# Four graph layers in one kernel: the third layer multiplies by its weights first, in fp32r halves, and by the triangles of the adjacency last

## What is computed

```python
def _layernorm(x, axis=-1, eps=1e-05):
    m = jnp.mean(x, axis=axis, keepdims=True)
    v = jnp.var(x, axis=axis, keepdims=True)
    return (x - m) / jnp.sqrt(v + eps)

def _L2_gnn_ref(x, W, adj, bias):
    adj_0 = jnp.diag(jnp.diagonal(adj))
    adj_1 = jnp.triu(adj, k=1)
    adj_2 = jnp.tril(adj, k=-1)
    h = jnp.einsum('bjf,kfo->kbjo', x, W)
    out = jnp.einsum('ij,bjo->bio', adj_0, h[0]) + jnp.einsum('ij,bjo->bio', adj_1, h[1]) + jnp.einsum('ij,bjo->bio', adj_2, h[2])
    return out + bias[None, None, :]
...
    h = jnp.maximum(_layernorm(x, axis=-1), 0.0)
    x = x + _L2_gnn_ref(h, L2_gnn_W, adj, L2_gnn_bias)
```

## Time and profile before

| | |
|---|---|
| median of three runs | 1389.29 us (1384.57 to 1389.65) |
| profiled execution | 1389.11 us, span 1387.3 us |
| busy PE / PEld / DVE / ACT / POOL over the span | 91% / 81% / 74% / 58% / 31% |
| third layer | from 912.7 to 1073.0 us of the span |

### The profile page before, as it was taken

One profiled execution on the slowest core, in us unless ns is written; L12 is line 12 of the kernel. 1 busy time (PEld: TensorE's weight loads), 2 busy tenths in 40 slices (PEclk: granted clock), 3 DMA queues, 4 the chain that ended last, 5 costly groups with the idle time before them and its releaser, 6 DMA issues. The chain is left out here.

```text
span 1387.3 us, 27428 instructions
## 1 busy us (share of the span) xinstructions
PE 1268.5 (91%) x8454; PEld 1123.1 (81%) x8454; DVE 1020.0 (74%) x2911; ACT 802.8 (58%) x1756; POOL 436.9 (31%) x546
## 2 busy tenths in 40 slices
PE   2899999999999999999997999979999899997998
PEld 2778787787877878778786877869998799985998
DVE  6677877778777787777875999967775688856675
ACT  3575775756757577575775777722221677752332
POOL 3121312213112131121311222268885333312332
PEclk7899999999999999999999999999999899987999
DMA  9200000000000000000000000000000000000222
GB/s 273 69 1 1 1 1 0 0 0 0 0 0 0 0 0 0 0 0 1 0 1 0 1 0 0 1 1 0 0 0 1 0 0 0 0 1 23 76 68 76
DMA packets 24696, 20.72 MB, mean 15 GB/s; under 512 B 1744, under 2 KB 20304, under 8 KB 24400
## 3 DMA queue, kind: packets, MB, share of 16 engines
q1 hardware_dynamic: 24656, 20.21, 5.1%
HBM read 11.82 MB, written 8.39 MB: 15 GB/s over the span
## 5 line engine op out<-in xcount | busy, mean ns | idle before, releaser
L579 ACT ACTIVATE gate<-ps,b_lstm 128x256 f32<-128x256 f32 (+2 forms) x624 | 300.8, 558 | 42.3 <-PE ps L606 42.0
L604 PE MATMUL ps<-H_hi,w_hi 128*128 128x256 f32 (+2 forms) x624 | 212.5, 342 | 30.0 <-ACT gate L579 18.2
L605 PE MATMUL ps<-H_hi,w_lo 128*128 128x256 f32 (+2 forms) x624 | 205.2, 330 | 0.0
L606 PE MATMUL ps<-H_lo,w_hi 128*128 128x256 f32 (+2 forms) x624 | 195.0, 333 | 6.7 <-DVE H_lo L548 6.5
L477 POOL TENSOR_TENSOR hid_lo<-hid,hid_hi 128x256 fp32r<-128x256 f32 (+2 forms) x96 | 88.1, 917 | 345.5 <-DVE hid L545 345.5
L604 PEld LDWEIGHTS ps<-H_hi,w_hi 128*128 128x128 f32 x624 | 117.5, 188 | 56.1 <-ACT gate L579 25.5
L589 ACT ACTIVATE tanh_c<-cell 128x512 f32<-128x512 f32 (+2 forms) x176 | 90.4, 514 | 124.0 <-DVE cell L538 82.8
L606 PEld LDWEIGHTS ps<-H_lo,w_hi 128*128 128x128 f32 x624 | 115.1, 189 | 22.5 <-DVE H_lo L548 10.3
L605 PEld LDWEIGHTS ps<-H_hi,w_lo 128*128 128x128 f32 x624 | 117.7, 189 | 7.9
L604 PE MATMUL ps<-hid_hi,w_hi 128*128 128x256 f32 (+2 forms) x384 | 119.1, 316 | 0.8 <-DVE hid_hi L544 0.8
L605 PE MATMUL ps<-hid_hi,w_lo 128*128 128x256 f32 (+2 forms) x384 | 117.3, 312 | 0.0
(11 more groups left out here) (199 smaller groups left out, 3295.6 us busy)
## 6 DMA issues: line engine op xcount, KB each, us to landing
out<-x SPq DMA_DIRECT2D x32, 256.0 KB, 2.3
w_raw<-in_WihT SPq DMA_DIRECT2D x1, 1024.0 KB, 8.3
w_raw<-in_WhhT SPq DMA_DIRECT2D x1, 1024.0 KB, 8.5
wqkvT<-in_WqkvT SPq DMA_DIRECT2D x1, 192.0 KB, 5.2
w_sb<-in_W SPq DMA_DIRECT2D x1, 192.0 KB, 4.8
ends_row<-in_src_row SPq DMA_DIRECT2D x1, 128.0 KB, 3.5
ends_row<-in_dst_row SPq DMA_DIRECT2D x1, 128.0 KB, 4.3
x<-in_x_in SPq DMA_DIRECT2D x8, 0.5 KB, 10.4
```

What stands on the lines that cost most here:

```text
L579: nc.scalar.activation(gate[:, g, z, 0:w * GB], gate_bank(g, k, m)[:, 0:w * GB], ACT.Tanh if z == G else ACT.Sigmoid, bias=b_lstm[:, 4 * ( ...
L604: nc.tensor.matmul(dst, w_hi[:, src, p - 1, z], v_hi, start=start, stop=False)
L605: return nc.tensor.matmul(dst, w_lo[:, src, p - 1, z], v_hi, start=False, stop=False)
L606: return nc.tensor.matmul(dst, w_hi[:, src, p - 1, z], v_lo, start=False, stop=stop)
```

## The change

The third layer is computed as adj x (h x W) instead of (adj x h) x W. For a group, TensorE transposes `hn` as before (stage HT2); ScalarE rounds its ReLU to `hT2_hi`, DVE makes `hT2_lo`. Stage MIX multiplies each transposed batch as stationary operand with the weights: three fp32r passes of 256 columns (both triangles' weights, into banks 4 and 5, `mix`) and three of 128 columns (the diagonal's weight, `own`), 24 instructions. ScalarE copies `mix` to `hw`, sorted by triangle. Stage OUT2 has the two triangles as stationary operands and all four batches of `hw` as 512 columns, in fp32. The diagonal is now a number for each partition (`diag_col`), which DVE multiplies with `own` and adds to `xb` (OWN) before the final add. Normalisation of the next turn moves: GpSimd makes scale and shift, ScalarE applies them with the ReLU in one instruction (APPLY2), as the fourth layer does; `hr` is gone. The order comes from `pipeline` with the list IN_TURN: HT2 and XB of group g, MIX and OWN of g-1, OUT2 of g-2, statistics and scale of g, APPLY2 of g-1. `hT2`, `hw`, `own` and the output have two buffers, `mix` has one. In setup, the three weights are split in halves (one instruction on ScalarE, one on DVE), and the matmul of ones with the diagonal goes. The tiles of the fourth layer's first block get a scope of their own, whose space the second block's tiles then use.

```diff
@@ setup @@
+                dve.wait_ge(S["w_high"], 4)
+                link(nc.vector.tensor_tensor(w2_lo[:], w2_sb[:].rearrange("p k o -> p (k o)"), w2_hi[:].bitcast(F32),
+                                             ALU.subtract))
...
-                link(nc.vector.tensor_copy(diag_bc[:], ps[:, 2, 0:P]))
+                link(nc.vector.tensor_reduce(diag_col[:], adj_diag[:], AXX, ALU.add))
...
+                nc.scalar.activation(w2_hi[:], w2_sb[:].rearrange("p k o -> p (k o)"), ACT.Copy).then_inc(S["w_high"], 1)
...
-                nc.tensor.matmul(ps[:, 2, 0:P], ones[:], adj_diag[:], start=True, stop=True)
@@ third layer @@
+        IN_TURN = [(HT2, 0), (XB, 0), (MIX, 1), (OWN, 1), (OUT2, 2), (STATS2, 0), (SCALE2, 0), (APPLY2, 1)]
+
+        def bank2(what, g):
+            return ps[:, {HT2: 0, OWN: 2, OUT2: 6}[what] + g % 2]
...
             def _(pool):
+                    elif what == SCALE2 and more:
+                        of = slice(g * QB, (g + 1) * QB)
+                        r, sh = rstd[:, of], shift[:, of]
+                        wait_apart(pool, S["c_aggr"], count * QB + QB)
+                        if before:
+                            wait_apart(pool, S["c_hn"], (count - W1 + 1) * QB)
+                        nc.gpsimd.tensor_scalar(r, mv[:, of, 1], EPS, None, ALU.add).then_inc(S["c_var"], 1)
+                        nc.gpsimd.tensor_scalar(sh, mv[:, of, 0], -1.0, None, ALU.mult).then_inc(S["c_nmean"], 1)
+                        pool.wait_ge(S["c_var"], count + 1)
+                        nc.gpsimd.tensor_tensor(r, r, half[:, 0:QB], ALU.pow).then_inc(S["c_rstd"], 1)
+                        pool.wait_ge(S["c_nmean"], count + 1)
+                        pool.wait_ge(S["c_rstd"], count + 1)
+                        nc.gpsimd.tensor_tensor(sh, sh, r, ALU.mult).then_inc(S["c_shift"], 1)
...
             def _(dve):
+                    if what == HT2:
+                        dve.wait_ge(S["c_hTh"], count + 1)
+                        nc.vector.scalar_tensor_tensor(hT2_lo[:, g % 2], by4(bank2(HT2, g)), 0.0,
+                                                       hT2_hi[:, g % 2].bitcast(F32),
+                                                       ALU.max, ALU.subtract).then_inc(S["c_hTl"], 1)
+                    elif what == OWN:
+                        own = xb[:, g * QB:(g + 1) * QB]
+                        dve.wait_ge(S["c_xb"], count + 1)
+                        dve.wait_ge(S["c_wp"], count + 1)
+                        nc.vector.scalar_tensor_tensor(own, by4(bank2(OWN, g)), diag_col[:], own,
+                                                       ALU.mult, ALU.add).then_inc(S["c_own"], 1)
+                    elif what == OUT2:
+                        dve.wait_ge(S["c_own"], count + 1)
+                        dve.wait_ge(S["c_op"], count + 1)
+                        nc.vector.tensor_tensor(x[:, bass.ds(i * NB + g * QB, QB), :], by4(bank2(OUT2, g)),
+                                                xb[:, g * QB:(g + 1) * QB], ALU.add).then_inc(S["c_o"], 1)
...
             def _(act):
+                    if what == HT2:
+                        act.wait_ge(S["c_hTp"], count + 1)
+                        nc.scalar.activation(hT2_hi[:, g % 2], by4(bank2(HT2, g)), ACT.Relu).then_inc(S["c_hTh"], 1)
+                    elif what == MIX:
+                        act.wait_ge(S["c_wp"], count + 1)
+                        if before or g > 1:
+                            act.wait_ge(S["c_op"], count - 1)
+                        nc.scalar.activation(hw[:, g % 2].rearrange("p k b o -> p b k o"),
+                                             ps[:, 4:6].rearrange("p a (b k o) -> p (a b) k o", b=2, k=2),
+                                             ACT.Copy).then_inc(S["c_hw"], 1)
+                    elif what == APPLY2 and more:
+                        act.wait_ge(S["c_hTp"], count + 1)
+                        act.wait_ge(S["c_shift"], count + 1)
+                        for j in range(g * QB, (g + 1) * QB):
+                            nc.scalar.activation(hn[:, j],
+                                                 x[:, bass.ds((i + 1) * NB + j, 1), :].rearrange("p a c -> p (a c)"),
+                                                 ACT.Relu, bias=shift[:, j:j + 1],
+                                                 scale=rstd[:, j:j + 1]).then_inc(S["c_hn"], 1)
...
             def _(pe):
+                    elif what == MIX:
+                        pe.wait_ge(S["c_hTl"], count + 1)
+                        if before or g > 0:
+                            pe.wait_ge(S["c_hw"], count)
+                        if before or g > 1:
+                            pe.wait_ge(S["c_own"], count - 1)
+                        for b in range(QB):
+                            mix = ps[:, 4 + b // 2, (b % 2) * 2 * C:(b % 2 + 1) * 2 * C]
+                            own = bank2(OWN, g)[:, b * C:(b + 1) * C]
+                            for dst, of in ((mix, slice(C, 3 * C)), (own, slice(0, C))):
+                                nc.tensor.matmul(dst, hT2_hi[:, g % 2, b], w2_hi[:, of], start=True, stop=False)
+                                nc.tensor.matmul(dst, hT2_hi[:, g % 2, b], w2_lo[:, of], start=False, stop=False)
+                                ins = nc.tensor.matmul(dst, hT2_lo[:, g % 2, b], w2_hi[:, of], start=False, stop=True)
+                        ins.then_inc(S["c_wp"], 1)
+                    elif what == OUT2:
+                        pe.wait_ge(S["c_hw"], count + 1)
+                        if before or g > 1:
+                            pe.wait_ge(S["c_o"], count - 1)
+                        for k in range(2):
+                            ins = nc.tensor.matmul(bank2(OUT2, g), adj_ul[:, k],
+                                                   hw[:, g % 2, k].rearrange("p b o -> p (b o)"),
+                                                   start=(k == 0), stop=(k == 1))
+                        ins.then_inc(S["c_op"], 1)
```

More of the change, by code:

```diff
@@ L714, in four_layers, with pipeline @@
         BESIDE = [(HT, 0), (PT, 2), (QK, 0), (VAL, 0), (EXP, 1), (SCORE, 0), (STATS, 0), (OUT1, 2), (APPLY, 1)]
-        def pipeline(engine, stage):
+        def pipeline(engine, stage, beside):
             def turn(i, first, last):
                 for step in range(W1):
-                    for what, behind in BESIDE:
+                    for what, behind in beside:
                         g = step - behind
@@ L730, in pipeline @@
             turn(TURNS - 1, False, True)
-            for step in range(max(behind for _, behind in BESIDE)):
-                for what, behind in BESIDE:
+            for step in range(max(behind for _, behind in beside)):
+                for what, behind in beside:
                     if behind > step:
@@ L920, in _ @@
+                pipeline(pool, stage, IN_TURN)
             @block.vector
             def _(dve):
[L922 to L928 removed]
@@ L930, in gather @@
-                def gather(i, g, more, before):
-                    dve.wait_ge(S["c_xb"], i * W1 + g + 1)
-                    dve.wait_ge(S["c_op"], i * W1 + g + 1)
-                    nc.vector.tensor_tensor(x[:, bass.ds(i * NB + g * QB, QB), :], by4(ps[:, 4 * (g % 2) + 3]),
-                                            xb[:, g * QB:(g + 1) * QB], ALU.add).then_inc(S["c_o"], 1)
-                    if more:
-                        dve.wait_ge(S["c_rstd"], i * W1 + g + 1)
-                        norm_apply((i + 1) * NB, g * QB, QB, S["c_hn"])
@@ L939, in aggr, with stage @@
-                def aggr(i, g, more, before):
-                    if more:
-                        wait_apart(dve, S["c_stats"], i * NB + (g + 1) * QB)
+                def stage(i, what, g, more, before):
+                    count = i * W1 + g
+                    if what == HT2:
[14 more added lines that the diff above has]
+                                                xb[:, g * QB:(g + 1) * QB], ALU.add).then_inc(S["c_o"], 1)
+                    elif what == STATS2 and more:
+                        norm_stats((i + 1) * NB + g * QB, 0, QB, S["c_stats"], g * QB)
+                        wait_apart(dve, S["c_stats"], count * QB + QB)
+                        if before:
+                            wait_apart(dve, S["c_shift"], count - W1 + 1)
@@ L942, in aggr, with stage @@
                         norm_aggr(g * QB, QB, S["c_aggr"])
-                def spread_and_aggr(i, g, more, before):
-                    spread(i, g, more, before)
-                    aggr(i, g, more, before)
-                one_behind(dve, spread_and_aggr, gather)
+                pipeline(dve, stage, IN_TURN)
             @block.scalar
             def _(act):
-                with act.Fori(0, TURNS) as i:
-                    for g in range(W1):
-                        act.wait_ge(S["c_zp"], i * W1 + g + 1)
-                        nc.scalar.activation(z12[:, g].rearrange("p b k t -> p (b k t)").rearrange(
```

(33 more changed lines are left out.)

97 lines of the change are left out of this document (40 added, 57 removed).

## The result

The changed kernel takes 1392.97 us (median of eight runs, 1388.33 to 1394.14) against 1387.64 for the kernel before (eight runs, 1384.57 to 1389.65). The ratio is 1.0035, with a 95% interval of 1.0021 to 1.0049: about 4.9 us slower, which is inside the 0.5% that the prediction counted as no change. The forecast was 1395.5, in a range of 1375 to 1408. The profiled execution took 1393.24 us, with a span of 1391.5.

A forecast was written before the change was run, and what follows sets the result against it. TensorE's time per group of the third layer was taken as the bound: 1389.1 + 5.1 (32 groups) + 1.0 (layer's start and end) + 0.5 (setup) = 1395.7, rounded to 1395.5 us, range 1375 to 1408.

The forecast's parts named there:

- What bounds the kernel: Third layer: TensorE's time per group, 4.85 us before, sets the price; other engines count only where they stop TensorE.
- The ring of the other engines: Third layer: chain through DVE, GpSimd, ScalarE and back, 4.2 us a group, under TensorE's 5.01, so costed at nothing.
- Short fp32r matmuls at 0.111, the unknown of the sum: Stage MIX, `own` product: each 128-column matmul costs its weight load, 0.111 us, so twelve make 1.34 a group; main case, 62%.
- the rival of cheap loads: Stage MIX: fp32r loads are cheap, a short matmul takes 0.059, a group 4.39, the kernel 1376 us; chance 19%.
- that of short fp32r at fp32's price: Stage MIX: short fp32r matmuls cost 0.223 each, a group takes 6.35, the kernel 1438 us; chance 12%.
- The test named for it: Profile after, L992 to L994: time between starts of 128-column matmuls, 0.11 if right, 0.06 or 0.22 if a rival holds.
- A group of 5.01: Third layer, TensorE per group: 0.44 + 0.09 + 1.41 + 1.34 + 1.73 = 5.01 us against 4.85, times 32 groups +5.1.
- the switch of type: TensorE, third layer: first fp32r matmul behind fp32 ones is followed after 0.21, not 0.118; 0.09 us once a group.
- The single `mix` buffer costs nothing, by 0.8 us: Before MIX: copy and hand-overs, 1.33, are covered by 2.17 of triangles and transposes; rival that it stops TensorE: 1402 us, 7%.
- The first, uncovered wait at the layer's start: Third layer's start: the second MIX waits 0.8 us for ScalarE's copy, not yet covered.
- Start and end +1.0: Third layer outside its groups: 6.1 us against 5.1 before, so +1.0.
- Setup +0.5: Setup: DVE's low part of the weights, 384 columns, lengthens the chain the first layer waits for at 37.37 by 0.5 us.

The follow-up runs named there:

- the plain fp32 version: Changed kernel with each batch's weights' product as one plain fp32 pass of 384 columns, no low part: 1381.22 us, ratio 0.9952 to the kernel before.
- the doubled copy: Changed kernel with ScalarE's copy of `mix` made twice for each group: 1399.73 us in one run (kernel before 1385.57).
- the memsets: Changed kernel with two DVE memsets of 1024 columns ahead of the fourth layer: 1395.6 us (before 1385.57); same added to the 384-column version: 1371.46 us.

## Why the prediction was right or wrong

**What bounds the kernel: right.** Every group of the layer's steady part takes the same 4.92, no other engine's work ends late enough to stop TensorE, and the price of the change is that of a group on TensorE. The ring of the other engines, put at 4.2 a group, didn't bind. With one short pass a group went down to 4.00, three of them 12.0; MIX, which is in the ring, is 0.9 longer in the changed kernel, so by an estimate from these numbers the ring is at most (12.0 + 0.9) / 3 = 4.3 there.

**Short fp32r matmuls at 0.111, the unknown of the sum: right.** Their price in place is (0.69 - 3 x 0.1178) / 3 = 0.112. Four columns cost as much as 128, and dropping eight matmuls with their loads saved 0.11 each. The price of the nearest row in mechanism, the logits in another type, held. This also rules out the rival of cheap loads (4.39 a group) and that of short fp32r at fp32's price (6.35). The test named for it was put wrongly, though: it asked for 0.11 between the *starts* of short matmuls, and those bunch behind the long ones (0.06, then 0.12 and 0.11); the rhythm is seen in the starts of the loads, or in the batch as a whole.

The Trainium skill, "TensorE: Matmul & The Clock Gate", section "Back-to-back issue gap", gives about 81 ns for a matmul of 128 columns with its load. These runs don't agree for fp32r: 112 ns, at full granted clock.

The Trainium skill, same page, section "Weight-path perf modes", switches its fast load on for 128 weights whose type isn't FP32, and gives fp32 weights no win from it. The loads of fp32r here start 0.11 to 0.12 apart, as the fp32 ones of the logits do, so these runs show no faster load for fp32r; whether the mode was off or brought nothing, they can't tell.

**A group of 5.01: 4.92 measured.** The triangles were 1.77 for 1.73, the twelve long and twelve short with their first interval 2.79 for 2.84. The transposes took 0.36 for 0.44. The sum had counted one delay twice: it kept the transposes' 0.44, which before reached to an fp32 matmul, and added 0.09 for the switch of type. In the plain fp32 version the transposes take 0.44 (984.31 to 984.75) and no switch follows; in the fp32r versions they take 0.36 and the first interval is 0.08 longer than the rest (0.20 against 0.12). Either way it is 0.44. Per layer, the error is 32 x 0.09 = 2.9 us.

**The single `mix` buffer costs nothing, by 0.8 us: right.** The copy took 1.02, not more for its strides, and the doubled copy showed the cover to be where the prediction put it: with about 2.1 us between the end of MIX and the next, two copies stop TensorE by 0.25 to 0.33. The first, uncovered wait at the layer's start was forecast at 0.8 and is 0.74:

```profile
916.12 0.58 PE L992 MATMUL ps<-w_hi,hT_hi 128*128 128x256 f32 x1 [0.56 <-DVE hT_lo L922]
...
922.00 0.36 PE L992 MATMUL ps<-w_hi,hT_hi 128*128 128x256 f32 x1 [0.74 <-ACT hw L956]
```

**Start and end +1.0: a little too much.** The first MIX came 2.5 after the first transposes (2.6 forecast) and lost 1.7 to the low level (4.5 less 2.8), where 2.2 was forecast. Outside 32 x 4.92 the layer has 5.4 to 5.7, against 5.1 to 5.4 before, so +0.3.

**Setup +0.5: wrong.** The step that failed is "on the chain that the first layer waits for at 37.37". DVE's chain was taken for the releaser because it ended late; the barrier waited for SyncE's issue of the last load, which the trace of before already showed ending at 36.68, later than DVE by 0.86. The size was right, DVE's chain did end 0.48 later in the changed kernel (36.30 for 35.82), but one more instruction on DVE moved nothing.

**The total.** Against the forecast of 1395.7, the groups account for -2.9, start and end for -0.7 and the setup for -0.8 (0.5 charged, 0.3 gained by SyncE's end in that run), which makes 1391.3. The profiled run stands at 1393.2; the +1.2 and +0.8 in the unchanged stages fill the difference, and these are within what they move by themselves. So the sum had its errors all on one side, 4.4 us together, small beside a range of 33 us. That the profiled run came as near as 2.3 us is in part luck: the 2.0 us of the unchanged stages, which no term forecast, hid about half of these errors. Nor was a change within 0.5% the likelier outcome by the prediction's own chances: 0.37, against 0.48 for slower. The main finding is where the expected gain of the hi/lo passes went: of three passes over 384 columns, 0.52 a batch, the split into 256 and 128 makes 0.69, because 24 loads pace the stage instead of twelve that hide.

## What to carry to other kernels

Count weight loads, not only columns: a 128x128 fp32 or fp32r load has a floor of about 0.11 us here, so an fp32r matmul of 4 or of 128 columns costs 0.11, almost the 0.118 of one with 256. Matmuls that share a stationary operand should have their moving operands side by side, even when their results go to different readers; here that turned a loss of 0.35% into a gain of 1.35%. Before an instruction is charged to the path in front of a barrier, look at what every engine, the issuing queue of SyncE too, does last before it.

## What the runs showed of the hardware that was not expected

The length of the low-clock stretch at the start of the third layer varied from 6 us (913.6 to 919.8 in the changed kernel) to 17 (912.1 to 929.1 with the memsets) between executions with the same code up to there, worth up to 4.7 us, although TensorE was at work nearly all the time from 916 to 928 in the longer one (4.00, 3.67 and 4.00 of each 4 us); the fourth layer took 308.4 and 313.9 us in two runs of one kernel, at granted clocks of 1.00 and 0.96. A comparison of single runs is therefore no finer than some 5 us for this kernel, and differences should be read inside a stage, by its period.

The floor of a load goes with the granted clock: at the low level six loads with their matmuls took 1.28 us (917.46 to 918.74 in the changed kernel), 0.21 each instead of 0.11 to 0.12. At the full clock an fp32r matmul of 384 columns takes 0.172 and one of 256 takes 0.118, which is 0.45 to 0.46 ns a column; an fp32 instruction of 384 columns takes 0.3225 (2.58 / 8), 0.84 ns a column, and a matmul has two of them. So three fp32r passes stand to one fp32 matmul as 0.517 to 0.645, a saving of a fifth at this width, with every load hidden.
